# First attention of a two-layer cross-attention and expert kernel: one visit of PE for a batch's value products, value rows made between the scores, stack rows by dimension

## The reference

```python
# 16 heads of 16 dimensions
qkv = x @ Wqkv + bqkv
qkv_a = xa @ Wqkv_aux + bqkv_aux
dots = einsum('bhqd,bhkd->bhqk', q, k) * scale        # 112 own keys
dots_aux = einsum('bhqd,bhkd->bhqk', q, ka) * scale   # 375 context keys
h_main = einsum('bhqk,bhkd->bhqd', softmax(dots), v)
h_aux = einsum('bhqk,bhkd->bhqd', softmax(dots_aux), va)
out = h_main * (1 - gate) + h_aux * gate
x = x + (out @ Wo + bo)
...
x = x + ffn0(layernorm(x))                 # 8 experts, the best of each row
x = x + attention1(ctx, ctx, layernorm(x)) # one head
x = x + ffn1(layernorm(x))                 # 16 experts, limited places
```

## Time and profile before

| | us |
|---|---|
| runs (three) | 779.21, 787.50, 787.95 |
| median | 787.5 |
| the profiled execution | 780.79 |
| its span | 779.1 |
| the first attention in it | about 447 |
| one step in the middle | 23.39 |

### The profile page before, as it was taken

How to read it: one execution, slowest core, us unless ns; L and a number is a source line. 1 busy time by engine, 2 the same in 40 slices (tenths; PEclk the granted TensorE clock), 3 DMA queues, 4 the chain that set the end, 5 groups by cost and what they waited for, 6 DMA issues and landing times. The chain is left out here.

```text
span 779.1 us, 19260 instructions
## 1 busy us (share of the span) xinstructions
PE 718.2 (92%) x6719; PEld 566.0 (73%) x6719; DVE 418.0 (54%) x1266; ACT 326.6 (42%) x883; POOL 217.8 (28%) x361
## 2 busy tenths in 40 slices
PE   3578999999999999998999789998999989999996
PEld 2445677766777666776667579997788868999994
DVE  2366777777777877776873323222588861111111
ACT  1316555566555566554555134441455541110110
POOL 3402331223321323321311113333355631111111
PEclk9959999999999999999999799999999998999998
DMA  5899977997888988888845638972566632999950
GB/s 156 95 167 118 179 112 118 134 121 130 139 146 145 168 101 145 145 144 109 103 136 176 169 119 237 292 214 74 180 194 212 217 100 81 311 337 335 332 170 16
DMA packets 98985, 128.15 MB, mean 164 GB/s; under 512 B 23362, under 2 KB 83883, under 8 KB 98768
## 3 DMA queue, kind: packets, MB, share of 16 engines
q1 hardware_dynamic: 90625, 115.24, 68.3%
q0 software_dynamic: 3824, 8.46, 4.1%
q10 hardware_dynamic: 4447, 3.30, 1.7%
HBM read 74.68 MB, written 23.88 MB: 127 GB/s over the span
## 5 line engine op out<-in xcount | busy, mean ns | idle before, releaser
L549 ACT ACTIVATE probs<-psum 128x448 f32<-128x448 f32 (+2 forms) x256 | 125.3, 541 | 59.2 <-PE psum L883 58.6
L755 DVE TENSOR_REDUCE neg_max<-psum 112x2 f32<-112x750 f32 x128 | 118.8, 928 | 7.5 <-PE psum L866 5.5
L866 PE MATMUL psum<-stacks 96*128 96x487 bf16 (+1 forms) x256 | 77.4, 385 | 8.8 <-DMA stacks<-q_parts 7.4
L883 PE MATMUL psum<-stacks 102*128 102x112 bf16 (+1 forms) x1024 | 77.1, 214 | 3.5 <-DVE c_wide L811 1.8
L898 PEld LDWEIGHTS psum<-probs,rings 128*32 128x32 f32 (+2 forms) x2048 | 45.0, 109 | 46.5 <-issue 37.7
L883 PEld LDWEIGHTS psum<-stacks 102*128 102x128 bf16 (+1 forms) x1024 | 54.2, 98 | 33.0 <-ACT probs L549 24.3
L898 PE MATMUL psum<-probs,rings 128*32 128x112 f32 (+2 forms) x2048 | 76.5, 265 | 1.4 <-issue 1.4
L1950 PEld LDWEIGHTS psum<-e_xt,rings 128*128 128x128 f32 x512 | 59.5, 192 | 2.2 <-ACT e_xt L1896 1.3
L1950 PE MATMUL psum<-e_xt,rings 128*128 128x112 f32 x512 | 59.7, 275 | 0.9 <-ACT e_xt L1896 0.9
L1916 DVE SCALAR_TENSOR_TENSOR e_y<-psum,e_x_in 112x256 f32<-112x256 f32 x16 | 7.7, 484 | 98.0 <-PE psum L1964 98.0
L1964 PE MATMUL psum<-rings,e_hid 128*112 128x256 f32 x256 | 57.9, 379 | 1.3 <-DVE e_hid L1923 1.3
(11 more groups left out here) (223 smaller groups left out, 1385.4 us busy)
## 6 DMA issues: line engine op xcount, KB each, us to landing
rings<-in_L_ffn_w SPq DMA_DIRECT2D x32, 1024.0 KB, 7.1
stacks<-rings SPq DMA_DIRECT2D x96, 243.5 KB
ct_dram<-rings SPq DMA_DIRECT2D x16, 375.0 KB, 10.8
a_ct<-ct_dram SPq DMA_DIRECT2D x16, 375.0 KB, 4.0
a_ctx<-in_ctx SPq DMA_DIRECT2D x16, 375.0 KB
stacks<-q_parts SPq DMA_DIRECT2D x96, 56.0 KB
rings<-in_ctx SPq DMA_DIRECT2D x16, 256.0 KB
w<-in_L_ffn_W SPq DMA_DIRECT2D x8, 512.0 KB, 11.4
```

What stands on the lines that cost most here:

```text
L549: nc.scalar.activation(probs[k % 4][0:keys, :, :], src, ACT.Exp, scale=DH ** -0.5).then_inc(s["exp_done"], 1)
L755: nc.vector.tensor_reduce(neg_max[:, 0, h:h + 2], psum[0:T, pair:pair + 2, 0:S], AX, ALU.max, negate=True)
L866: last = nc.tensor.matmul(bank[2 - 2 * (k % 2) + j][0:rows, 0:KV], q_flat[n.third][0:QK, h * T:h * T + rows], k_stack[n.third][0:QK, h, :] ...
L883: last = nc.tensor.matmul(bank[4 + k % 2][0:wide, j * T:(j + 1) * T], k_flat[n.third][:, first:first + wide], q_stack[n.third][:, h, :], s ...
```

## The change

Six things change, all in attention0.

1. The value products of a batch (L898, now L935) stand in one visit behind all eight pairs, for the batches 0 to 13. The last two batches keep the old order. For this each of the 16 slots has its own tile of probs: five of its own, two in free room, and nine in the half of w1 that belongs to the experts 4 to 7.
2. The value rows of batch b-2 are made in the front, one of the eight matmuls behind each pair of scores (make_values, L951), into banks 6 and 7. Before, they were those of batch b-1, made in the back. ACT copies the first part behind exp of slot 9 and the rest behind exp of slot 15. The last batch still has its value rows made in the back of step 16, into banks 0 and 1.
3. On PE the choice's turn goes behind that of the maxima, and the second half of the keys (keys_of(b, 1)) goes ahead of the choice's score and of turn_back.
4. On ACT the copy of the maxima and its DMA go ahead of copy_in, and high_k(b, 1) ahead of mixed.
5. On DVE norm of the choice goes from the fifth pair to behind the split of the maxima, and the layer norm of the next batch ahead of normalise.
6. SP writes a term to the stack rows t, t+6, ..., t+90, and the experts 4 to 7 of W1 are loaded in step 16, when the probs tiles in them have been read.

```diff
@@ attention0, tiles
-        probs = [sb(f"probs{k}", [P, 4, T]) for k in range(4)]
+        probs = [sb(f"probs{k}", [P, 4, T]) for k in range(5)]
+        probs += [early([P, 4, T]) for _ in range(2)]
+        late_w1 = g_.w1[:, EARLY_W1:E0, :, :].rearrange("p e k f -> p (e k f)")
+        probs += [late_w1[:, k * 4 * T:(k + 1) * 4 * T].rearrange("p (j q) -> p j q", j=4) for k in range(9)]
+        def v_bank(n):
+            return 0 if n.c == B - 1 else 6
@@ SP
             def copy_terms(b, part):
                 for t in range(NT):
-                    rows = slice(DH * t, DH * t + DH)
+                    rows = slice(t, QK, NT)
...
-                if FIRST <= b.c < FIRST + E0:
+                if FIRST <= b.c < FIRST + EARLY_W1:
                     load_expert(b - FIRST)
+                if b.c == B:
+                    sp.wait_ge(s["pv_done"], 16 * LAST_APART)
+                    for e in range(EARLY_W1, E0):
+                        load_expert(Item(0, e, E0))
@@ ACT
                         act.wait_ge(s["logits_mm"], n.count(16, k + 1))
-                        act.wait_ge(s["pv_done"], n.count(16, max(k - 3, 0)))
+                        if n.c >= LAST_APART:
+                            act.wait_ge(s["pv_done"], n.count(16, max(k - 3, 0)))
...
+                        if k == 9 and b.c <= B:
+                            values_of_first(b - 2)
+                if (b - 2).real() and b.c <= B:
+                    if not (b - 3).real():
+                        values_of_first(b - 2)
+                    values_of_rest(b - 2)
@@ PE
             def values(n, k):
                 g, c = k // 4, k % 4
                 pe.wait_ge(s["exp_done"], n.count(16, k + 1))
-                if k in (0, 8) and (n - 1).real():
-                    pe.wait_ge(s["mixed_ready"], (n - 1).count(2, k // 8 + 1))
+                if k in (0, 8):
+                    if n.c < LAST_APART:
+                        pe.wait_ge(s["v_ready"], (n + 1).count(3, 1 + k // 4))
+                    else:
+                        pe.wait_ge(s["mixed_ready"], (n - 1).count(2, k // 8 + 1))
...
+            def make_values(n, k):
+                c, h = k // 2, k % 2
+                at = v_bank(n)
+                if k in (0, 4) and n.c < B - 1 and (n - 2).real():
+                    pe.wait_ge(s["mixed_ready"], (n - 2).count(2, 1 + k // 4))
+                if c < 3:
+                    lo, keys = CHUNKS[c]
+                    to, left, right = bank[at + c // 2][0:keys, c % 2 * D:(c % 2 + 1) * D], ct[n.parity][:, h, lo:lo + keys], w_aux[:, h, D:2 * D]
+                else:
+                    to, left, right = bank[at + 1][0:T, D:2 * D], xt[n.parity][:, h, :], w_x[:, h, 2 * D:3 * D]
+                made = nc.tensor.matmul(to, left, right, start=(h == 0), stop=(h == 1))
...
+                last_ones = (b - 3).real() and (b - 3).c >= LAST_APART
                 for pair in range(8):
                     if (b - 3).real():
                         logits(b - 3, 2 * pair)
                         logits(b - 3, 2 * pair + 1)
                     if (b - 2).real():
                         max_scores(b - 2, pair)
-                    if (b - 3).real():
-                        if pair >= 1:
-                            values(b - 3, 2 * pair - 2)
-                            values(b - 3, 2 * pair - 1)
-                if (b - 3).real():
+                    if (b - 2).real() and b.c <= B:
+                        make_values(b - 2, pair)
+                    if last_ones and pair >= 1:
+                        values(b - 3, 2 * pair - 2)
+                        values(b - 3, 2 * pair - 1)
+                if last_ones:
                     values(b - 3, 14)
+                elif (b - 3).real():
+                    for k in range(16):
+                        values(b - 3, k)
```

More of the change, by code:

```diff
@@ L602, in step @@
                     high_k(b, 1)
+                if (b - 3).real():
+                    mixed_out(b - 3, 0)
+                    mixed_out(b - 3, 1)
+                if b.c == B + 2:
+                    pad(act, range(3))
+                if b.real():
                     act.wait_ge(s["qk_mm"], b.count(1, 1))
@@ L774, in step @@
                     nc.vector.tensor_tensor(max_parts[:, :, 2, :], max_rest[:, :, :], max_parts[:, :, 1, :], ALU.subtract).then_inc(s["msplit"], 1)
+                if (b - 4).real():
+                    r.norm(dve, b - 4, xs)
+                if (b + 1).real():
+                    ln(b + 1)
                 if (b - 3).real():
@@ L1009, in step @@
                                         ident16[0:T, 0:T]).then_inc(s["mt_mm"], 1)
+                if (b - 4).real():
+                    if (b - 3).real():
+                        pe.wait_ge(s["exp_done"], (b - 3).count(16, 15))
+                    r.turn(pe, b - 4, ident)
+                if last_ones:
+                    values(b - 3, 15)
                 if (b - 3).real():
@@ L1014, in step @@
                         g_.keep_busy(bank[2], 2)
-                if (b - 1).real():
-                    n = b - 1
-                    if b.real():
-                        pe.wait_ge(s["xt_ready"], b.count(1, 1))
-                        pe.wait_ge(s["ct_ready"], b.count(2, 1))
-                    else:
-                        pe.wait_ge(s["max_done"], (b - 2).count(8, 8))
-                    for c in range(2):
-                        for h in range(2):
-                            last = nc.tensor.matmul(bank[0][:, c * D:(c + 1) * D], ct[n.parity][:, h, c * P:(c + 1) * P],
-                                                    w_aux[:, h, D:2 * D], start=(h == 0), stop=(h == 1))
-                    last.then_inc(s["v01_mm"], 1)
-                    for h in range(2):
-                        nc.tensor.matmul(bank[1][0:CHUNKS[2][1], 0:D], ct[n.parity][:, h, 2 * P:S], w_aux[:, h, D:2 * D],
-                                         start=(h == 0), stop=(h == 1))
-                    for h in range(2):
-                        last = nc.tensor.matmul(bank[1][0:T, D:2 * D], xt[n.parity][:, h, :], w_x[:, h, 2 * D:3 * D],
-                                                start=(h == 0), stop=(h == 1))
-                    last.then_inc(s["v23_mm"], 1)
+                if b.c == B:
+                    pe.wait_ge(s["max_done"], (b - 2).count(8, 8))
+                    for k in range(8):
+                        make_values(b - 1, k)
+                if b.real():
+                    pe.wait_ge(s["xt_ready"], b.count(1, 1))
+                    pe.wait_ge(s["ct_ready"], b.count(2, 2))
+                    if (b - 2).real():
+                        pe.wait_ge(s["mt_ready"], (b - 2).count(1, 1))
+                    if not b.looped() and b.c == 0:
+                        pe.wait_ge(s["w_made"], 6)
+                        pe.wait_ge(s["bias_ready"], 1)
+                    keys_of(b, 1)
                 if (b - 4).real():
```

84 lines of the change are left out of this document (35 added, 49 removed).

## The result

The changed kernel takes 754.8 us, the median of five runs (750.6 to 764.2), against 785.2 for five runs of the kernel before (779.2 to 788.0). The ratio is 0.9605, with a 95% interval of 0.9551 to 0.9659: 30 us faster. It leaves out the run of 764.2 as a slow one. The forecast was 768, so the gain is nearly twice the one that was forecast, and the time lies near the lower end of the range, 752 to 786.

What follows compares the result with a forecast made beforehand. PE was taken to set the step. Thirteen steps gaining 0.8 us each (-10.4), the start (-7) and the end (+2) gave -15.4 us, set against a mean of 783.9: forecast 768 us, range 752 to 786.

Steps and rivals of the forecast that it cites:

- rival 4: More than forecast: no switch ahead of the value matmul, back hides all, pair at 1.28; about 757 us; chance 0.16.
- The visit: Value products of a batch on PE: one visit costs 3.33 us instead of 4.24 for eight, 0.91 us out.
- Rival 3: One visit of 64 products runs at the pace of mixed work, 2.6 us more a step, about 802 us; chance 0.07.
- The pair: Front of a steady step: logits 0.40, scores 0.51 and a value row matmul 0.43 make 1.34 us, eight 10.7.
- rival 1: Slots bounded by the exponentials or by switches, steady gain becomes a loss of 0.2, about 781 us; chance 0.13.
- Rival 2: Maxima arrive late by the DMA of mt, each step loses 0.7 us, about 777 us; chance 0.09.
- The copy behind exp 9: ACT's copy of the first value rows makes exp 10 0.23 late; PE waits about 0.15 us, once.
- The back: Without value rows the back grows by 0.2 us to 8.3, bounds 8.1 and 8.9.
- +2.5, -3.46: Steady step: front and value products grow by 2.5 us, value rows leaving the back save 3.46, 1.0 gained.
- The start: First steps: 7 us gained, between 1 and 9; 3 from a sooner first stack, 3.46 + 0.56 from step 2's back.
- The end: Step 16 makes two batches' value rows, +2 us; the late half of W1 costs nothing, steps 17 and 18 keep their order.
- the spread rows do nothing: Spread stack rows don't bring the first stack sooner: 3 us less gain, 771.5 us, within the forecast's own range.

Runs made afterwards that it cites:

- e6: Changed kernel with one more wait, on a semaphore long reached, ahead of each of the eight value row matmuls; ratio 0.960.
- e7: Kernel before without the waits for the exponentials ahead of the value products of slots 0 to 13; ratio 0.998.
- e0: The changed kernel run and profiled again, nothing changed; ratio 0.961, span 748.5 us.
- e5: Changed kernel with the second half of the keys behind turn_back on PE and high_k behind mixed on ACT, as before; 770.8 us, ratio 0.986.
- e4: Changed kernel with DVE's old order: norm of the choice in the fifth pair, layer norm behind normalise; 767.3 us, ratio 0.977.
- e8: Kernel before with the value products in one visit and the spread stack rows, value rows still in the back; 786.9 us, ratio 1.0056.
- e2: Kernel before with only the stack rows changed, to t, t+6, ..., t+90; 777.7 us, ratio 0.993.
- e1: Changed kernel with the old stack rows, 16t to 16t+15 for term t; 816.5 us, ratio 1.043.
- e3: Kernel before with the value products in one visit, old stack rows, value rows still in the back; 838.3 us, ratio 1.071.
- e9: Changed kernel with a term's 16 stack rows at every second partition instead of every sixth; ratio 0.959.
- e11: Changed kernel with 18.9 MB more HBM to HBM transfers on SP's queue, behind the stack copies of steps 4 to 15; ratio 0.962.

## Why the prediction was right, and where it was not

The time inside the range owes something to the range's width. The measured 754.8 is rival 4's time (757), to which the prediction gave 0.16, and not its own 768.

**What bounds the kernel** was read rightly: PE, before and after, and the gain is PE's time.

**The visit.** 3.33 by the slope of a slot, 3.22 measured. Rival 3, that a run of 64 products would be slower than one of 12, is refuted by every quiet step.

**The pair** was mis-sized: 1.34 forecast, 1.25 measured. The scores were carried over with the 0.51 that they take ahead of the value products, and take 0.42 ahead of the value rows. The text named this as rival 4's first condition. e6 and e7 show that the 0.09 is no matter of waits. It goes with the change to 32 columns. With the 0.13 a visit there is a cost at both sides of a visit, and the sum took away only one of the two. It's paid once in the new step, by the last value row. ACT's chain was put at 1.28 and didn't hold the pair at 1.25, where ACT idles 0.27. Eight pairs make 0.7 us a step, 9 us in all. This is the largest error in the sum of a step (1.62 against 0.8). It also settles rival 1, which had the pair grow. Rival 2, the maxima late, didn't come either: no step of e0's profile waits for the DMA of mt.

**The copy behind exp 9** was to cost 0.15. In e0's profile as in the first one, the fifth pair takes 1.40 and the others 1.25.

**The back** was put at 8.3 and is 8.23. The wait ahead of the keys, 0.2 forecast, is there. Their first weights are loaded late, 0.1 after ACT's copy of the maxima has ended (297.27):

```profile
297.38 0.93 PEld L1008 LDWEIGHTS psum<-rings 128*128 128x128 f32 x4 [0.26 <-issue]
```

PE's own row shows no idle time, but its first keys matmul starts 0.31 behind the last turn of pv, where the turns are 0.11 apart, so 0.20 is lost.

The margins read for turn_back and the choice were real and thin: with either reorder undone (e5, e4) 1.26 to 1.36 us of a step come back, so of the 1.62 gained, nearly all hangs on each of them.

**The two moves need each other.** The visit alone makes a step 0.77 longer (e8), since the front is then held by DVE's maxima at 9.57. With the value rows in it the front is 10.32. So 3.46 us of matmuls cost 0.75 there. This is where most of the gain comes from, and the prediction's sum of it (+2.5, -3.46) had it right in kind.

**The start**: 7 forecast, 8.2 measured, by the steps given: the first maximum at 37.7 for 38.5, and PE at half clock for a part of step 2's front. **The end**: +2 forecast, +1.9 measured for steps 16 and 17, but 1.2 of it in step 17, which was taken as unchanged. There the turn of the maxima waits 1.50 for DVE's split, 0.83 before. Another 1.8 came behind step 17, for which the sum had no term, and its cause stays open. So the end cost 3.7.

**The step that failed** is the sentence that in the steady steps the spread rows give nothing, since PE has no wait for the stacks there. That PE has no named wait there was true, and not enough. The kernel before lost 4 to 5 us to stops that the wait list calls issue (e2), and with the visit in place the old rows lose 65 (e1). The forecast of 771 for the case that the spread rows do nothing was off for the same reason: 816. The prediction had written down 23.7 as the mean of 13 steps and 23.39 for one of them, and didn't ask for the difference. It was a cost that the change was about to multiply.

Two rules of the Trainium skill were weighed. By the map of SBUF — State Buffer, Door 1: The DMA port swizzle, 16 neighbouring rows lie four to a port and the spread ones at most two, and the share of 0.90 that became 0.51 with the same bytes (e2) agrees. That of TensorEngine Tiling (Array Packing), Key Properties, that a change of the tiling mode drains TensorE, agrees with the 0.09 and the 0.13 at the two sides of a visit.

**What the stops are.** They are PE's code arriving late, and three counts in the traces show it.

- The place. Count the records of PE in a trace, matmuls, weight loads and the few others. All 38 stops named issue in the steps 3 to 17 stand, in eleven of the fourteen profiles, at the same place of a block of 256 records, give or take one. In e1 the distances from one to the next are 512, 1279, 512, 513, 1280, 511, 513, 511, 1281 and 512.
- The time. Each of the 38 ends 1.3 to 2.0 us after the end of a 16 KB packet of the instruction queue q8.
- The order. In the first 430 us of each of the 14 profiles these packets pair off with the blocks of 256, one each, in order. PE never begins a block sooner than 1.27 us after its packet has ended. In e2, which has no stop, the smallest distance is 4.2 us, and in e0 it is 1.6, in step 7, and 1.9 in step 3. So the changed kernel has little room in these two steps, and there all the single stops of it and its variants with spread rows fall (0.4 to 3.1 us).

That the visit makes the stops larger fits this: its 128 matmul records and as many weight loads are one whole block in 3.22 us, where a step of 21.77 has some 570 records.

**What stays open** is why the packets are late when the queue holds copies of neighbouring rows (e1, e3) and not with spread ones or with other traffic (e2, e8, e9, e11). What the traces add is the backlog: the copy of ct to DRAM, issued on SP's queue behind the stack copies, lands after 10.2 to 10.6 us with the old rows and after 3.7 to 4.2 with the new.

## What to carry to other kernels

When matmuls move between phases, add up the phase they enter by its own limit, not by theirs: in a phase held by another engine they are almost free, and taking work out of it gains nothing. A stop named issue while DMA is full is a cost with a cause, even if no one waits for that DMA's data. Look for an instruction packet that ends just before the stop does, ask which transfers are slow, and try their rows spread over the partitions. And read each pair of neighbours for the cost of the switch between them before a sum reuses a duration.

## What the runs showed of the hardware

- Copies into 16 neighbouring partitions ran at about 115 GB/s, the same bytes into every sixth or every second partition mostly at 180 to 300, with DMA's share of a step 0.47 in both (the changed kernel, e9).
- PE's code came in packets of 16 KB, one for 256 of PE's recorded instructions. PE went on 1.3 to 2.0 us after the end of one that it had to wait for (38 stops, up to 6.8 us long, in eleven profiles).
- A stop of 6.16 us let the granted clock fall, and the next 4.5 us of PE work had 0.64 of it (e1).
- A wait on a semaphore already reached, eight times a step ahead of a matmul, added nothing that shows in 0.01 us of a pair (e6).
- 64 products of 32 by 112 in float32 in a row took 3.22 us, 0.05 each (the changed kernel).
